# A router rebuilt inside a fused transformer kernel: scores taken before the layer norm, token lists built by scattered writes

## The reference

```
# gated layer
q, k, v = x @ Wq.T + bq, x @ Wk.T + bk, x @ Wv.T + bv
g = sigmoid(x @ Wg.T + bg)
x = layernorm(x + q * cumsum(k * v, axis=tokens) * g)
# mixture: 32 experts, D_FF 192
p = softmax(x @ gate_weight.T);  top, idx = top_k(p, 8)
w = top / sum(top)
prim, sec = idx[:, :4], idx[:, 4:]
# each secondary choice goes to the most similar primary (sim has ones on its diagonal),
# unless that similarity is below 0.5
new_sec = where(max(sim[sec, prim]) < 0.5, sec, prim[argmax(sim[sec, prim])])
combine = sum(one_hot([prim, new_sec]) * w)
y = sum over experts e of (silu(x @ g_e) * (x @ u_e)) @ d_e * combine[:, e]
x = layernorm(x + y)
```

## Time and profile before

| what | us |
|---|---|
| median of 3 runs | 1586.79 (1586.19 to 1589.04) |
| the profiled execution | 1585.89 |
| its span, first to last instruction | 1584.0 |
| gated layer, first to last projection's end | 666.65 to about 871 |
| router's tail, last projection to tables_ready | about 871 to 951.1 |
| experts, first gather to last scatter | 952.1 to 1548 |
| mean granted TensorE clock | 0.961 |

### The profile page before, as it was taken

One profiled execution on the slowest core, in us unless ns is written; L12 is line 12 of the kernel. 1 busy time (PEld: TensorE's weight loads), 2 busy tenths in 40 slices (PEclk: granted clock), 3 DMA queues, 4 the chain that ended last, 5 costly groups with the idle time before them and its releaser, 6 DMA issues.

```text
span 1584.0 us, 33491 instructions
## 1 busy us (share of the span) xinstructions
PE 1448.3 (91%) x11191; PEld 820.2 (52%) x11192; DVE 952.9 (60%) x1858; ACT 732.3 (46%) x1326; POOL 776.5 (49%) x691
## 2 busy tenths in 40 slices
PE   5999999999999999999998358999999999999990
PEld 2566666544444444445454215666666666666650
DVE  7877777776757666634988883444444444444435
ACT  6544433555464645444446442444444444444443
POOL 3565544530010202044445536777777777777655
PEclk9999999999999999999999668999999999999995
DMA  6323111269776868531101444888989898876767
GB/s 242 107 81 107 27 40 26 77 219 315 238 255 232 265 222 268 179 139 54 55 3 54 158 165 93 185 183 166 202 177 206 177 196 186 162 108 96 177 76 230
DMA packets 102991, 243.45 MB, mean 154 GB/s; under 512 B 21481, under 2 KB 23049, under 8 KB 101904
## 3 DMA queue, kind: packets, MB, share of 16 engines
q1 hardware_dynamic: 67312, 183.08, 35.0%
q0 software_dynamic: 35616, 59.58, 23.0%
HBM read 158.92 MB, written 101.71 MB: 165 GB/s over the span
## 4 chain that ended last, share of the span: by engine, by line
PE 68%; DVE 16%; issue 6%; POOL 4%; ACT 3%; DMA 2%; SPq 0%; DVEq 0%; POOLq 0%; ACTq 0%
PE bank L894 20%; PE bank L915 11%; PE bank L562 8%; PE bank L706 6%; PE bank L712 6%; PE bank L735 6%; PE bank L885 5%; PE bank L904 2%; ACT ARENA L1395 1%; POOL ARENA L1695 1%; DVE ARENA L1032 1%; POOL ARENA L1690 1%; DVE ARENA L1266 1%; DVE ARENA L985 1%; PE bank L551 1%
## 5 line engine op out<-in xcount | busy, mean ns | idle before, releaser
L894 PE MATMUL bank<-ARENA,XT 128*128 x1908 | 364.2, 327 | 2.2 <-issue 1.1
L1826 POOL DMA_INDIRECT accs<-X,WA x159 | 252.5, 1588 | 98.8 <-issue 34.7
L894 PEld LDWEIGHTS bank<-ARENA,XT 128*128 128x128 f16 x1908 | 180.4, 98 | 124.2 <-issue 8.2
L1356 DVE COPY XT<-bank 128x1024 f16<-128x1024 f16 x159 | 109.9, 691 | 182.3 <-PE bank L885 181.1
L1819 POOL DMA_INDIRECT XT<-x_rows,WA x159 | 166.5, 1047 | 87.0 <-issue 39.8
L1395 ACT ACTIVATE ARENA<-ARENA 128x512 f16<-128x512 f32 (+2 forms) x128 | 89.3, 709 | 245.5 <-DVE ARENA L1114 134.1
L915 PE MATMUL bank<-ARENA,XT 128*128 x795 | 197.4, 379 | 0.9 <-issue 0.9
L1649 ACT ACTIVATE XT<-bank 128x192 f32<-128x192 f32 x159 | 52.5, 330 | 287.7 <-PE bank L894 287.7
L562 PE MATMUL bank<-XT,STG 128*128 128x512 f16 x640 | 151.8, 385 | 4.6 <-DVE ARENA L1160 4.3
L1677 POOL TENSOR_TENSOR rstd<-mv,mhalf 128x1 f32<-128x1 f32 x28 | 8.7, 309 | 258.2 <-DVE mv L964 258.2
L1395 ACT ACTIVATE XT<-bank 128x384 f16<-128x384 f16 (+2 forms) x207 | 125.7, 607 | 9.5 <-PE bank L551 9.0
(11 more groups left out here) (245 smaller groups left out, 2369.6 us busy)
## 6 DMA issues: line engine op xcount, KB each, us to landing
w_scratch<-WA SPq DMA_DIRECT2D x64, 640.0 KB, 3.9
ARENA<-w_scratch SPq DMA_DIRECT2D x64, 640.0 KB
ARENA<-w_exp SPq DMA_DIRECT2D x48, 640.0 KB, 5.2
WA<-w_exp SPq DMA_DIRECT2D x16, 640.0 KB, 5.1
ARENA<-ARENA SPq DMA_DIRECT2D x64, 128.0 KB, 2.3
accs<-ARENA SPq DMA_DIRECT2D x20, 256.0 KB, 3.1
X<-x SPq DMA_DIRECT2D x4, 1024.0 KB, 6.6
ARENA<-wc SPq DMA_DIRECT2D x8, 512.0 KB, 6.0
```

The source lines that it names most:

```text
L894: mm = pe.matmul(d, xTb[k.u % 2][:, a * KD + kd, :], weights(sl, b, kd * 2 * DFF, 2 * DFF), start=(a, b, kd) == (0, 0, 0), stop=(a, b, kd) ...
L1356: dve.tensor_copy(xTb[k.u % 2].rearrange("p c n -> p (c n)"), bank[k.u % 2][:, :].bitcast(F16)).then_inc(xt_sb, 1)
L1826: pool.indirect_dma_start(accs, bass.IndirectOffsetOnAxis(blkout[:, i:i + 1], 0), yD[i % 8], None, compute_op=ALU.add).then_inc(y_out[i % ...
```

## The change

- **Scores.** The router's scores are now made from the input of the gated layer's residual and from its output before the norm (`input_logits`: as before 48 f16 matmuls of 32 columns, on the old x; `layer_logits`: four f32 matmuls in each step on aC), both into bank 3. The mean is subtracted with the help of the column sums of the gate weights (`gate_sums`, `csneg`), and the softmax is taken over the eight chosen scores alone, scaled by rstd. So the transposes of the normed tiles fall away for the batches 0 to 3 of this layer (`norm_transposes` and `norm_copy` stay only for the last batch of the layer before).
- **Products.** POOL makes only qC * cumC, and DVE the product with gC, at the head of the next step.
- **Choices among experts.** One-hots of both the primary and the secondary choices are transposed (8 f32 transposes in place of 4), and multiplied so that DVE finds the nearest primary by six passes over 512 elements in place of eight such passes, sixteen small ones and two of 1024.
- **Lists.** `places` makes one number for each choice, and POOL writes the token number to its place in a list in memory by an indirect DMA of 128 elements of 4 bytes: 32 such `dispatch` DMAs for each of the batches 0 to 2. Batch 3 still goes by one-hots (32 values of 159 columns on DVE, 21 positions on DVE and 11 on ACT) and 32 matmuls. Two indirect DMAs read the list back, and two matmuls add it to the table.
- **Weights of batch 3.** The combination for batch 3 is made on POOL (products of 1024, sums of 512, 256 and 128 elements).
- **Expert weights.** All `load_expert` come after the scores of batch 3 and its stored rows; experts 1 to 7 come after `store_weights(3)`.
- Constants come in two transfers, the zeros for the sums in four.

The core of the diff:

```diff
@@ SP
-            sp.wait_ge(onehot_used, 2 * TB * TOPK)
-            load_expert(0)
             store_weights(2)
             store_rows(3)
-            for e in range(1, 4):
-                load_expert(e)
             sp.wait_ge(logit_ready, BATCH)
             for tt in range(TB):
                 sp.wait_ge(xr_out[tt], 16 * BATCH)
-            sp.wait_ge(acc_init, 16 * (2 * ROWS // P))
-            load_expert(4)
+            sp.wait_ge(list_zero, 16 * 2)
+            sp.wait_ge(acc_init, 16 * (4 + NT))
+            load_expert(0)
             store_weights(3)
-            for e in range(5, NSLOT):
+            for e in range(1, NSLOT):
                 load_expert(e)
@@ PE
+            def layer_logits(s):
+                for tt in range(TB):
+                    mm = pe.matmul(bank[3][:, tt * EXPERTS:(tt + 1) * EXPERTS], aC[:, s % 2, tt * P:(tt + 1) * P], gw32[:, s % KD, :],
+                                   start=False, stop=s % KD == KD - 1 and tt == TB - 1)
             def similarities(b):
-                pe.wait_ge(ohT_sb, b + 1)
+                pe.wait_ge(ohT_sb, 2 * b + 2)
                 for tt in range(TB):
-                    mm = pe.matmul(bank[6][:, tt * P:(tt + 1) * P], ohT[:, tt, :], bdsim[:, :], start=True, stop=True)
+                    pe.matmul(bank[6][:, tt * P:(tt + 1) * P], primT[:, tt, :], prio[:, 0:P], start=True, stop=False)
+                    pe.matmul(bank[6][:, tt * P:(tt + 1) * P], ohT[:, tt, :], bdsim[:, :], start=False, stop=True)
+                    mm = pe.matmul(bank[7][:, tt * EXPERTS:(tt + 1) * EXPERTS], primT[:, tt, :], prio[:, P:P + EXPERTS], start=True, stop=True)
@@ PE, the steps
                 gate_proj(s, 1)
+                if et == 1:
+                    if q >= 1:
+                        choice_transposes(q - 1)
+                    input_logits(q)
+                if et == 2 and q >= 1:
+                    ranks(q - 1)
                 gate_proj(s, 2)
                 if s > 0:
                     back(s - 1)
+                    layer_logits(s - 1)
+                if et == 1 and q >= 1:
+                    similarities(q - 1)
                 gate_proj(s, 3)
-                if et == 2 and q >= 1:
-                    logits(q - 1)
-                if et == 3 and q >= 2:
-                    slot_sums(q - 2)
@@ DVE
+            def product(s):
+                dve.wait_ge(gc_sb, s + 1)
+                dve.wait_ge(a1_ready, s + 1)
+                dve.tensor_tensor(aC[:, s % 2, :], a1C, gC, ALU.mult).then_inc(a_ready, 1)
+            def exponents(b):
+                dve.wait_ge(ln_rstd, 2 * NT + (b + 1) * TB)
+                ...
             for s in range(BATCH * KD):
+                if s > 0:
+                    product(s - 1)
+                if et == 1 and q >= 1:
+                    exponents(q - 1)
                 running_sum(s)
@@ ACT, in step et == 1
-                    for tt in range(TB):
-                        high_half(q, tt)
+                    if q >= 1:
+                        exponentials(q - 1)
+                    high_half(q, 0)
+                    high_half(q, 1)
+                    if q >= 1:
+                        second_copy(q - 1)
+                        first_copy(q - 1)
+                    high_half(q, 2)
+                    high_half(q, 3)
@@ POOL
+            def dispatch(b, lo, hi):
+                ...
+                for i in range(lo, hi):
+                    t = b * TB + i // TOPK
+                    pool.indirect_dma_start(slot_list, bass.IndirectOffsetOnAxis(places_i[b][:, i:i + 1], 0), pay[:, t:t + 1], None,
+                                            bounds_check=EXPERTS * TOK - 1, oob_is_err=False).then_inc(list_out, 16)
             for s in range(BATCH * KD):
+                if et == 0 and q >= 2:
+                    dispatch(q - 2, 14, 20)
+                if et == 1 and q >= 1:
+                    norm_shifts(q)
+                if et == 2 and q >= 2:
+                    dispatch(q - 2, 28, 32)
+                if et == 3 and q >= 1:
+                    dispatch(q - 1, 4, 10)
                 product(s)
+                if et == 0 and q >= 2:
+                    dispatch(q - 2, 20, 24)
+                if et == 1:
+                    low_halves(q)
+                if et == 1 and q >= 2:
+                    dispatch(q - 2, 24, 28)
+                if et == 2 and q >= 1:
+                    dispatch(q - 1, 0, 4)
+                if et == 3 and q >= 1:
+                    dispatch(q - 1, 10, 14)
+            dispatch(2, 14, 18)
+            norm_shifts(BATCH)
+            dispatch(2, 18, 24)
+            low_halves(BATCH)
+            dispatch(2, 24, 32)
+            pool.wait_ge(wts_ready, BATCH)
+            pool.wait_ge(mask_ready, BATCH)
+            ...
+            pool.wait_ge(list_ready, BATCH + 1)
+            pool.wait_ge(list_out, 16 * (BATCH - 1) * ROWS_B)
+            for g, rows in enumerate((P, NBLK - P)):
+                pool.indirect_dma_start(listed[0:rows, g, :], None, list_rows, bass.IndirectOffsetOnAxis(listidx[0:rows, g:g + 1], 0),
+                                        bounds_check=LISTROWS - 1, oob_is_err=False).then_inc(list_in, 16)
```

More of the change, by code:

```diff
@@ new lines, in ranks, with slot_sums @@
+                mm = pe.matmul(d, ones, before[b].rearrange("p t e -> p (t e)"), start=False, stop=not last)
+                if not last:
+                    mm.then_inc(rank_ready, 1)
+            def slot_sums():
+                for i in range(ROWS_B):
+                    if i % 3 == 0:
+                        pe.wait_ge(row_act, i // 3 + 1)
+                    pe.wait_ge(onehot_ready, i + 1)
+                    pe.matmul(bank[7][:, 0:NBLK], oneR[i], oneV[i][:, 0:NBLK], start=i == 0, stop=False)
@@ L876, in _ @@
-            mm.then_inc(blk_ready, 1)
+            pe.matmul(bank[3][0:1, 0:EXPERTS], nb[0:EXPERTS, 0:1], upper[0:EXPERTS, :], start=True, stop=True).then_inc(count_ready, 1)
+            pe.wait_ge(count_sb, 2)
+            for tt in range(TB):
+                mm = pe.matmul(rank_bank[:, tt * EXPERTS:(tt + 1) * EXPERTS], ones[0:EXPERTS, :], startrow[0:EXPERTS, :],
+                               start=False, stop=tt == TB - 1)
+            mm.then_inc(rank_ready, 1)
+            pe.wait_ge(count_sb, 3)
@@ new lines, in _ @@
+            for g in range(2):
+                pe.matmul(bank[5][:, 2 * g:2 * g + 2], ended[0:EXPERTS, g * P:(g + 1) * P], perblock[0:EXPERTS, :], start=True, stop=True)
+            pe.matmul(bank[4][0:1, 0:NBLK], ones[0:EXPERTS, 0:1], ended[0:EXPERTS, 0:NBLK], start=True, stop=True)
+            pe.matmul(bank[2][:, 256:256 + NBLK], alternate[0:EXPERTS, :], ended[0:EXPERTS, 0:NBLK], start=True, stop=True).then_inc(count_ready, 1)
+            slot_sums()
+            pe.wait_ge(list_in, 16 * 2)
@@ new lines, in places, with block_places @@
+                step(dve.tensor_tensor(key, key, mask, ALU.mult))
+                for t in range(TB):
+                    own.did(dve.max(place8[:, t, :], key[:, t, :]))
+                own.settle()
+                dve.tensor_scalar(places_i[b], place8.rearrange("p t r -> p (t r)"), -1.0, float(EXPERTS * TOK), ALU.mult, ALU.add).then_inc(list_ready, 1)
+            def block_places():
+                dve.wait_ge(rank_ready, BATCH)
+                step(dve.scalar_tensor_tensor(key, ranks, 1.0, mask, ALU.add, ALU.mult))
+                for t in range(TB):
+                    own.did(dve.max(place8[:, t, :], key[:, t, :]))
+                own.settle()
+                step(dve.tensor_scalar(rhi, place8, -64.5, 1 / P, ALU.add, ALU.mult))
@@ L1255, in places, with one_hots @@
+                own.did(dve.tensor_scalar(rneg, rlo, -1.0, None, ALU.mult))
+                step(dve.tensor_scalar(vcol, rhi, 1.0, None, ALU.add))
                 dve.memset(idle[:, :], 0.0).then_inc(list_ready, 1)
-                step(dve.tensor_scalar(coef, coef, 0.0, None, ALU.is_gt))
-                step(dve.scalar_tensor_tensor(vcol, vcol, 1.0, coef, ALU.add, ALU.mult))
-            def one_hots(b, lo=0, hi=TB * TOPK):
-                for i in range(lo, hi):
+            def one_hots():
+                for i in range(ROWS_B):
@@ L1322, in _ @@
-            one_hots(3, 0, 8)
-            dve.wait_ge(rows_ready, 1)
+            own.did(dve.scalar_tensor_tensor(endc[one, :], pos1[one, :], spare[one, :], bank[2][one, 0:1], ALU.mult, ALU.add))
+            step(dve.tensor_scalar(cnt[one, :], nb[one, 0:1], spare[one, :], None, ALU.add))
+            step(dve.tensor_scalar(first[one, :], endc[one, :], cnt[one, :], float(P), ALU.subtract, ALU.mult))
+            dve.tensor_scalar(startrow[one, :], ident16[one, 0:EXPERTS], first[one, :], None, ALU.mult).then_inc(count_sb, 1)
@@ new lines, in _ @@
+            own.did(dve.tensor_copy(perblock[one, 1:2], cnt[one, :]))
+            step(dve.tensor_scalar(ended[one, :], iotab[one, :], endc[one, :], None, ALU.is_ge))
+            dve.memset(idle[:, :], 0.0).then_inc(count_sb, 1)
```

(3 more changed lines are left out.)

565 lines of the change are left out of this document (258 added, 307 removed).

## The result

| | us, median (range) | span of the profiled run |
|---|---|---|
| before | 1587.67 (1586.19 to 1589.04) | 1584.0 |
| after | 1603.92 (1599.10 to 1605.27) | 1597.2, executed in 1599.1 |

The ratio is 1.0097, with a 95% interval of 1.0074 to 1.0121: slower by 1%, where I had forecast 0.5% faster. The profiled run is the fastest of its four, 4.8 us under their median; where the other three lose these, no trace tells.

The account below looks back on a forecast made before the run. POOL was to bound the kernel from about 755 to the table: last product at 895, plus 48.6 us of tail, table at 943.5 against 951.1, 7.6 us saved, hence 1579 us; range 1555 to 1606.

Parts of the forecast that it names:

- d: POOL's time for one dispatch in the gated layer and tail: taken as 1.25 us, break-even at 1.34.
- rival 2: POOL, step 9 to the table: a dispatch costs like the adding scatter, 1596 to 1633 us; chance 0.21.
- The sum to the last product: Gated layer: POOL's 140 us of work and idle from 755 put the end of product(15) at 895, before 877.2.
- POOL's idle before the products of steps 9 and 13: Gated layer, batch ends: POOL idles 8.5 us while ACT works through to qC, for q = 2 and q = 3.
- PE's waits before `similarities`: Gated layer: PE waits for ACT's copies, 3 to 9 us in batch 2 and 9 to 13 in batch 3.
- The tail: After product(15): POOL's chain takes 48.6 us, table at 943.5; DVE's chain 42.4 plus up to 7.
- my fourth case: Experts' stage: loads of eight experts hold PE up, one expert late costs some 5 us, 1584; chance 0.04.
- Behind the table: From the table on: gathers start as before and the experts' stage keeps its length to 2 us.
- The slope of 0.84 us for each 0.01 of d: Whole time: 96 dispatches and two list reads, less about 14 hidden behind PE, move the forecast by this much.
- Cheap dispatches: Gated layer and tail: d near 1.05 without a gap, table at 927, 1562 us; chance 0.22.
- Fewer stalls at batches' ends: Gated layer: ACT's copies come early, so batch-end stalls shrink, 8 us back, 1571 us; chance 0.08.
- A dispatch costs like the adding scatter: The same as rival 2: the adding scatter takes 1.59 us, 1.89 with a gap, and all wait for POOL; chance 0.21.

Follow-up runs that it names:

- e6_dve_product: Changed kernel with the product qC*cumC of all 16 steps moved from POOL to DVE: 1596.03 us.
- e1: Changed kernel without the list entries of every token's last four choices, 48 of the 96 dispatches left out: 1562.51 us, ratio 0.985.
- e2: Changed kernel with six dispatches of a batch moved between the shifts and the product, in steps with et = 1: 1595.93 us.
- e3: Changed kernel with ACT's two copies of the choices ahead of its exponentials and high halves: 1598.03 us.
- e5: Changed kernel with expert 0 loaded behind the routing weights of batch 3, like the other experts: 1600.27 us.
- e4: Changed kernel with experts 0 to 3 loaded in the gated layer and 4 to 7 behind the last batch's weights: 1597.72 us.
- e8: Changed kernel with product on DVE, ACT's copies ahead of the exponentials, experts 0 to 3 loaded in the gated layer: 1567.82 us; repeated in another sitting, 1595.89.
- e10: Changed kernel with six scatters ahead of the product, ACT's copies ahead of the exponentials, experts 0 to 3 loaded in the gated layer: 1588.09 us.
- b1: Kernel before, with only the changed order of the experts' loads (none before the last batch's rows are stored): 1586.65 us, ratio 0.9998.
- e9: Changed kernel with each of the 96 scatters writing 16 rows instead of 128, lists mostly empty: 1581.48 us, ratio 0.9973.

## Why the prediction was wrong

**The size of d.** This is the first step that failed, the term of the sum for a dispatch; the second is a term put at nothing, the landing in the tail below. I took 1.25, measured are 1.40; I had put the break-even at 1.34 and the slower side, rival 2, at 0.21. The floor was right: 0.97 + 0.30 = 1.27, nearly the gather's 1.30. What I left out is that the dispatches run beside a working DVE. 19 of the 96 last over 1.1 us, 12.0 us more than 19 of the others, and each of them starts while DVE is in a pass over two operands in SBUF. All 25 that start inside such a pass end 0.78 to 1.13 us behind its end. The 71 that start in none took 0.97 to 0.98, also the 10 among them that start inside a pass of 512 elements with one operand in PSUM. One such pass beside the dispatch at 773.35 shown above, and the one-hot comparison beside that at 782.00, which lasts 2.01:

```profile
773.29 1.22 DVE L1180 TENSOR_TENSOR_SCAN ARENA<-ARENA 128x512 f32<-128x512 f32 x1
...
781.94 1.23 DVE L1225 TENSOR_TENSOR WA<-WA 128x1024 f32<-128x1024 f32 x1
```

The dispatch at 773.35 ends at 775.30, 0.79 us after the pass (774.51), nearly as if it had begun then. Six more of 1.50 stand behind a POOL product, where DVE's L1205 has just started 0.69 us of work that the product released. In the other direction it is POOL's passes, not its dispatches, that hold DVE up. DVE's one-hot columns, 0.31 us each in the tail, took 2.83 for two beside POOL's combination, and its comparison L1251 took 3.93 beside the low halves. In e6_dve_product the same comparison takes 0.69 in the three batches where POOL is in no such pass, in two of them beside a dispatch:

```profile
929.67 3.93 DVE L1251 TENSOR_TENSOR WA<-WA 128x512 f32<-128x512 f32 x1
...
942.56 2.83 DVE L1297 TENSOR_SCALAR STG<-WA 128x159 f16<-128x159 f16 x2
```

I had weighed the Trainium skill (SBUF — State Buffer, section "SBUF: two separate sides") only for the one-hots and dropped it by the 5% between gathers. The same section says that a DVE instruction with two SBUF inputs and a GpSimd instruction that reads SBUF exclude each other for the whole instruction. The trace agrees for a dispatch behind such a pass, with 1.95 instead of 0.97 us, and not for a pass behind a dispatch, by the 0.69 just named. The two dispatches beside one-hot columns took 0.97, so that part of my doubt fits. That the passes are the cause is read from overlap in time, in all 19 cases and in none of the 71; no run took the passes away alone.

**The sum to the last product.** Forecast 895, measured 905.4. The sum's 74 dispatches times 0.15 give 11.1, the whole of it. First dispatch 754.86 (755 forecast). POOL's idle before the products of steps 9 and 13: 7.94 and 7.95 (8.5). PE's waits before `similarities` 11.16 and 6.68; I had 3 to 9 and then 9 to 13, so the order was reversed, and it was luck that the sum of the two lies inside. e1, and less strongly e2 and e3, agree with POOL and the chain at the batch's end setting the pace together.

**The tail.** POOL from there to its last dispatch: 38.0 us (37.6 forecast), the combination 4.7 (4.9). Not foreseen was the landing: I counted 2.1 us for the reads and nothing for the scatters ahead of them, taking the landing of a gather in an empty stretch for all. Behind expert 0's load it is 6.40; e5, e4, e8 and e10 give 1.34, 1.42, 1.09 and 2.36 without it. That POOL's chain would end the tail, with DVE's some microseconds ahead of it, came true: it was 3.0. In my fourth case the weights cost 5 us, but in the experts' stage. The price was there, the place was wrong: a move that costs nothing on the kernel before (b1) costs it here. The table: 943.5 forecast, 962.0 measured, 18.5 = 10.4 + 6.4 + 1.7, the last in the reads and small terms.

**Behind the table.** 635.2 us against 632.9: 2.3, forecast as the same to 2. Together 1578.3, the forecast of one execution, + 18.5 + 2.3 = 1599.1, what the profiled run took. I had put the median 0.9 over it, and it is 4.8 over it. Where these are lost, no trace shows; in the profiled run PE's unexplained waits are 2.5 us, and whether the other runs had more isn't known.

**Slips in the working.** The slope of 0.84 us for each 0.01 of d leaves out 14 dispatches that my sum counts: the sum goes up by 0.98, which puts the break-even near 1.33. The experts take 596 of 1584 us, 38%, not 59%. Neither moves the forecast.

**Rivals.** "Cheap dispatches" falls by the 0.30 between every two. "Fewer stalls at batches' ends" falls by 7.94 and 7.95. "A dispatch costs like the adding scatter" fell as to price (1.40, not 1.59 + 0.30) and held as to mechanism: POOL is the engine that all wait for, and the break-even of 1.34 was passed, though by DVE's passes beside it.

**What beats the kernel before.** Product on DVE, copies first and experts 0 to 3 early: 1.1% faster in one sitting (0.9893, 0.9877 to 0.9910) and 0.7% slower in another (1.0070, 1.0049 to 1.0091). It isn't a version to take before TensorE's unexplained waits are understood. The kernels that leave work out beat it too (e1, e9), but don't count.

## What to carry to other kernels

Price an instruction of POOL by its row beside a working DVE, and look up which of DVE's passes read two tiles in SBUF: a dispatch that began inside one here lasted until 0.8 to 1.1 us behind its end. An indirect DMA of single words cost POOL 1.15 to 1.3 us with its gap, for 16 as for 128 of them, so count them before giving lists to scatters. When a wait for small DMAs is moved to the end of a chain, look at what large load is under way at that moment, and at which chain ends next if the wait goes. And run the kernel that you compare with in the same sitting: small gains over a median from another one aren't shown.

## What the runs showed of the hardware that was not expected

- A scatter's time on POOL hardly depends on its rows: 0.846 us for 16, 0.974 for 128, with 0.30 to the next in both.
- A dispatch that started inside a pass of DVE over two operands in SBUF lasted up to 2.03 us instead of 0.97; the passes themselves kept their 0.69 us beside a dispatch, but took up to 3.93 beside POOL's low halves.
- Words of 4 bytes issued by 943.4 had landed only at 954.5, with 2 transfers of 640 KB beside them; without these POOL waited 1.1 to 2.4 us instead of 6.4.
- TensorE can stand in straight code with no release that the profile shows. These waits, 700 to 906: none in two kernels of the old routing, 0 to 6.9 us in ten of the new one with the product on POOL, and with the product on DVE 0, 18.1, 15.7 to 19.1 and 26.1 to 29.8 in four sittings. The granted clock was 0.67 in such a stretch. The blocks of code follow TensorE's place and don't explain them. What does, and why one sitting had none in four kernels (at most 0.8 us), stays open.
